# Earlier row counts, eight more 128-row tiles and moved matmuls in a recurrence fused with a mixture of experts

## The reference: what is computed

```python
xW = einsum('ntd,dh->nth', x, Wx) + b              # x: 2 sequences, 1024 steps, 256 wide
h[t] = tanh(xW[t] + h[t-1] @ Wh)                   # 1024 steps, one after the other
logits = h.reshape(2048, 256) @ gate_w.T           # 8 experts
top_v, top_i = top_k(logits, 2); probs = softmax(top_v)
for e in range(8):                                 # inner width 1024
    hidden = silu(h @ wg[e].T) * (h @ wu[e].T)
    out += combine[e] * (hidden @ wd[e].T)         # combine is 0 where e was not chosen
return x + out
```

## Time and profile before

| what | value |
|---|---|
| median of three runs | 864.16 us |
| the profiled execution's own time | 867.19 us |
| its span, first to last instruction | 865.4 us |
| TensorE matmuls busy | 803.9 us, 93% of the span |
| granted TensorE clock, mean | 0.903 |
| loads of expert rows (two for a pair) | 86 |

### The profile page before, as it was taken

How to read it: one execution, slowest core, us unless ns; L and a number is a source line. 1 busy time by engine, 2 the same in 40 slices (tenths; PEclk the granted TensorE clock), 3 DMA queues, 4 the chain that set the end, 5 groups by cost and what they waited for, 6 DMA issues and landing times.

```text
span 865.4 us, 53138 instructions
## 1 busy us (share of the span) xinstructions
PE 803.9 (93%) x22592; PEld 773.2 (89%) x22592; DVE 455.6 (53%) x2595; ACT 537.1 (62%) x2864; POOL 154.0 (18%) x142
## 2 busy tenths in 40 slices
PE   7777777899999999999999999999999999998994
PEld 4666666799999999999999999999999999998994
DVE  4677676545545454545454544545454545455552
ACT  4777787556666666666665666666665666654552
POOL 1001001010301121110302030212222131314332
PEclk7555555599999999999999999999999999999998
DMA  6667667411111111111201120112111111112211
GB/s 174 169 183 195 181 173 197 152 29 22 36 22 29 27 32 28 29 26 19 42 15 35 22 41 16 31 27 34 24 26 27 23 31 20 30 24 40 33 28 24
DMA packets 36021, 50.07 MB, mean 58 GB/s; under 512 B 5808, under 2 KB 22448, under 8 KB 35760
## 3 DMA queue, kind: packets, MB, share of 16 engines
q1 hardware_dynamic: 27408, 36.93, 15.5%
q0 software_dynamic: 8384, 9.84, 8.2%
HBM read 35.71 MB, written 13.14 MB: 56 GB/s over the span
## 4 chain that ended last, share of the span: by engine, by line
PE 81%; DMA 6%; DVE 4%; ACT 4%; issue 3%; SPq 0%; DVEq 0%; POOLq 0%; ACTq 0%
PE bank L506 27%; PE bank L424 18%; PE bank L583 15%; PE bank L528 13%; DMA arena<-w_all 4%; PE bank L537 3%; ACT h L746 3%; DVE lo L1044 3%; PE bank L403 2%; PE bank L485 1%; DMA out<-y_sb,place_now 1%; PE bank L477 1%; ACT w_hi L731 1%; DVE w_lo L1019 1%; PE bank L446 0%
## 5 line engine op out<-in xcount | busy, mean ns | idle before, releaser
L1044 DVE TENSOR_TENSOR lo<-h,hi 128x4 f16<-128x4 f32 x1024 | 168.2, 164 | 355.1 <-ACT h L746 339.4
L738 ACT ACTIVATE hi<-bank 128x4 f16<-128x4 f32 x1024 | 177.5, 173 | 230.6 <-PE bank L424 201.1
L583 PE MATMUL bank<-lo,wh_hi 128*128 128x2 f16 x4096 | 258.1, 167 | 29.8 <-DVE lo L1044 26.5
L424 PE MATMUL bank<-hi,wh_hi 128*128 128x2 f16 x4096 | 251.8, 165 | 10.6 <-ACT hi L738 9.3
L424 PE MATMUL bank<-hi,wh_lo 128*128 128x2 f16 x4096 | 245.6, 163 | 0.8 <-issue 0.8
L583 PEld LDWEIGHTS bank<-lo,wh_hi 128*128 128x128 f16 x4096 | 174.9, 99 | 45.8 <-DVE lo L1044 42.5
L424 PEld LDWEIGHTS bank<-hi,wh_hi 128*128 128x128 f16 x4096 | 200.0, 99 | 17.8 <-ACT hi L738 12.4
L746 ACT ACTIVATE h<-bank 128x4 f32<-128x4 f32 x1024 | 178.1, 174 | 32.8 <-PE bank L583 29.7
L424 PEld LDWEIGHTS bank<-hi,wh_lo 128*128 128x128 f16 x4096 | 177.7, 97 | 1.0 <-issue 0.9
L506 PE MATMUL bank<-x_T,w_hi 128*128 128x64 f16 (+1 forms) x2304 | 168.6, 202 | 2.2 <-DVE arena L972 1.5
L506 PE MATMUL bank<-x_T,w_lo 128*128 128x64 f16 (+1 forms) x1152 | 154.1, 202 | 0.0
(11 more groups left out here) (140 smaller groups left out, 1208.8 us busy)
## 6 DMA issues: line engine op xcount, KB each, us to landing
arena<-w_all SPq DMA_DIRECT2D x96, 256.0 KB, 2.9
xrow<-expert_rows SPq DMA_DIRECT2D x86, 66.0 KB
early<-xT SPq DMA_DIRECT2D x16, 128.0 KB, 2.9
expert_rows<-pad SPq DMA_DIRECT2D x1, 1056.0 KB, 8.6
expert_rows<-rows,slot POOLq DMA_INDIRECT x64
out<-y_sb,place_now POOLq DMA_INDIRECT x36, 3.2
out<-y_sb,place_wide POOLq DMA_INDIRECT x24
arena<-wh_in SPq DMA_DIRECT2D x1, 256.0 KB, 2.9
```

The source lines that it names most:

```text
L424: mm = pe.matmul(preact(n)[:, B * m:B * m + B], w[:, k, m * P:(m + 1) * P], hi[:, blk % 2, k, B * tt:B * tt + B], start=False, stop=False, ...
L583: mm = pe.matmul(preact(n)[:, B * m:B * m + B], wh_hi[:, k, m * P:(m + 1) * P], lo[:, pi, k, B * pt:B * pt + B], start=False, stop=False, ...
L738: act.activation(hi[:, blk % 2, :, B * tt:B * tt + B], src, ACT.Tanh, scale=1 / SCALE).then_inc(s_hi, 1)
L1044: v.tensor_tensor(lo[:, i, :, B * tt:B * tt + B], h32[:, 4 * (tt % 2):4 * (tt % 2) + 4].rearrange("p (c b) -> p c b", c=2), hi[:, i, :, B ...
```

## The change

The count of a block moves from 4 steps behind its last scatter to 3 steps ahead of it, and the scatters move to o = 0, 3, 6 and 9. `WIDE` becomes 32, so that pairs 24 to 31 take 128 rows of one expert. `fewer` is worked out from `heavy`: a step with a turn of x or y, or with logits or turned rows, hands two units (one 128-column matmul, or two of 64) to the other step of its couple (n ^ 1), unless that one is heavy too. The slice of pair 35 is made in the last four steps. In the tail the last count and routing ticks come one job later, and the list in lots of 3, 3 and 2.

```diff
--- before.py
+++ after.py
@@ -35,14 +35,14 @@
 TICKS = 19
 START, PERIOD, HALF_T = 208, 24, 12
 R = 64
-WIDE = 24
+WIDE = 32
 UNITS, FIRST_UNITS, FIRST_STEPS = 14, 24, 6
 SILU_AT, HI_AT = (2, 8), (5, 11)
 MUL_AT, LO_AT = (4, 10), (6, 0)
 YT_AT, WEIGH_AT, X_OUT_AT = 12, (15, 18), (21, 22)
 Y_TURN_AT, X_TURN_AT = (13, 14), (19, 20)
 SLICE_AT, TAKE_AT, SHIFT_AT, PASS_AT = (7, 8, 9, 11), 19, (13, 14), 15
-ADD_AT, SCATTER_AT = (16, 22), (2, 5, 9, 12)
+ADD_AT, SCATTER_AT = (16, 22), (0, 3, 6, 9)
 EXTRA = 2
 
 
@@ -103,7 +103,7 @@
         return [m for m in range(n, n + 2 * PERIOD) if (m - START) % PERIOD in SCATTER_AT][:4]
 
     def count_step(blk):
-        return scatter_steps(blk)[3] + 4
+        return scatter_steps(blk)[3] - 3
 
     def slice_step(p):
         return START + (p - 1) * PERIOD + SLICE_AT[0]
@@ -538,11 +538,14 @@
                               start=False, stop=True, skip_group_check=True)
                     n -= 4
 
-            def tile(p, o):
+            def heavy(n):
+                return pair_of(n)[1] in Y_TURN_AT + X_TURN_AT or (n >= STEPS and n % STEPS in (0,) + TURN_ROWS_AT)
+
+            def tile(p, o, n):
 
                 half, w = divmod(o, HALF_T)
                 part, sub = divmod(w, 2)
-                fewer = HALF_T - 2 if o in Y_TURN_AT else HALF_T + 2 if o in (Y_TURN_AT[0] - 1, Y_TURN_AT[1] + 1) else HALF_T
+                fewer = HALF_T + 2 * (heavy(n ^ 1) - heavy(n))
                 n0, n1 = (2 * HALF_T - fewer, 2 * HALF_T) if sub else (0, fewer)
                 pq, hq = (p, 0) if half else (p - 1, 1)
                 t = pq if part in (2, 5) else p
@@ -585,7 +588,7 @@
                 mm.then_inc(s_pre, 1)
                 units = 0
                 if p >= 0:
-                    units += tile(p, o)
+                    units += tile(p, o, n)
                 if not last:
                     units += next_xw(blk, tt)
                 if blk:
@@ -1062,6 +1065,8 @@
                         route(1 - i, blk - 1, tick)
                     if n == count_step(blk):
                         count(blk - 1)
+                if n >= T - 4:
+                    make_slice(NPAIR + 1, n - (T - 4))
 
             v.memset(all1[:], 1.0).then_inc(s_c, 1)
             v.memset(seen[:], 0.0).then_inc(s_c, 1)
@@ -1133,15 +1138,14 @@
             hidden_lo(NPAIR - 1, 1, 1)
             for tick in range(3, 14):
                 route(1, g, tick)
-            whole_slice(NPAIR + 1)
 
             def count_and_place(n):
-                if n == 1:
+                if n == 2:
                     count(g)
                     for tick in range(15, 20):
                         route(1, g, tick)
-                if n >= 2:
-                    lists(2 * n - 4, 2 * n - 2)
+                if n >= 3:
+                    lists((0, 3, 6)[n - 3], (3, 6, 8)[n - 3])
 
             def list_and_slice(n):
                 if n == 0:
```

## The result

The changed kernel takes 845.03 us (median of four, 843.07 to 846.02) against 863.79 us for the kernel before, a ratio of 0.9777 (95% interval 0.9755 to 0.98). Run again on another chip it took 844.14 us against 865.05, 0.9757 (0.9743 to 0.977). The prediction was 843.5 us, range 839 to 850. By medians the gain is 18.8 us the first time and 20.9 the second. The profiled execution took 846.02 us, 21.2 us less than the profiled one of before; the sum of terms had been 21.3.

The account below looks back on a forecast made before the run. TensorE's instruction stream was taken as the bound, with narrow code arriving too slowly. Terms 9.5 + 7.1 + 4.2 + 0.5 = 21.3 us gave 842.9 us against the median; a little less gain was taken: 843.5 us, range 839 to 850.

Parts of the forecast that it names:

- The sum: Whole kernel: 9.5 + 7.1 + 4.2 + 0.5 = 21.3 us less, taken as 843.5 us.
- What bounds the kernel: Whole kernel: TensorE's instruction stream, 81% of the chain of waits; narrow code is used up faster than it arrives.
- Part 1: Tail loop: by the count of rows five pairs in place of six, 84 loads for 86, saving 9.5 us.
- Part 2: Pairs 24 to 31 made wide: 6.3 us less there, 0.8 us in pairs 32 and 33, together 7.1 us.
- Part 3: Couples of steps hand a product over: turns of x, turned rows and logits shorten, 4.2 us together.
- fixed stock of 41 us: Narrow stretch: a stock of code carries it about 41 us before the first stall; pairs 32 and 33 need 35.
- "seventeen" steps: Pairs 26 to 31 of the kernel before: seventeen stalled steps above 0.88 us, many some 4.1 us apart.
- Part 4: Tail's order: times_up(34, 0, 1) ahead of last count and ticks, slice of pair 35 into steps; 0.5 us together.
- 0.4 us of the slice: Slice of pair 35, 0.9 us of VectorE, moves into steps; 0.4 us of it lay on the path.
- Part 5: Early count: in eight blocks load_pair waits for the last scatter's landing, but the load stays hidden by 1.5 us.
- The rival's price: Load late in eight periods: 851.5 us at 1 us late, slower than before above 2.6 us each; 5%, 2% slower.
- one of the prediction's signs of being wrong: Step o = 19, first reader of the expert rows: TensorE or VectorE waiting there for the load.

Follow-up runs that it names:

- the last run: Changed kernel with scatters at o = 0, 2, 4 and 6 and the last slot copy in a tick 20, run once more: 843.61 us, ratio 0.9739 to the kernel before.

## Why the prediction was right, point by point

**The sum.** That 21.3 met the 21.2 of the profiles so closely is in part luck. The steps from pair 1 on gave 11.8 us against 11.3, the tail 10.4 against 10.0, and the 1.0 us lost ahead of pair 1 stood in no term.

**What bounds the kernel**: TensorE's stream of instructions. Doubling the matmuls of eight pairs, and with them the weight loads, brought the stalls back, 8.3 us, and they end with the arrival of code. The Trainium skill, "Runtime: NRT & Kernel Launch", section "Instruction fetch mechanics", calls the crossing of a block mostly hidden. The traces agree for the wide code here (TensorE idle 0.02 us in 138.76) and not for the narrow (2.90 us in 105.06).

**Part 1, one pair fewer, 9.5 us**: right. The count from the routing gave 84, 88 and 84 loads for the three kernels that it was asked for. Beside the pair, the other pairs of the loop came 9.32 us apart in place of 9.46; with the rest of the tail that made 10.4. Why the spacing fell wasn't found: it is 9.27 to 9.39 us in the profiles with the narrow pairs, without the handover, with the late count and with the old tail too, so none of these makes it alone.

**Part 2, 7.1 us**: right in size, with part 3's share taken off: 7.5 - 1.0 in pairs 24 to 31, and 1.2 less 0.24 behind them. But what narrow code costs differs between kernels: 146.24 us in the kernel before, 143.34 with the pairs narrow again. Its premise of a fixed stock of 41 us was wrong: pairs 32 and 33 had no step above 0.86 us in the changed kernel, but stalls of 0.35 and 0.4 us, among others, in the last run. Of the "seventeen" steps above 0.88 us the starts of L746 show sixteen.

**Part 3, 4.2 us**: right, 4.05 in the traces, and of the 144 steps in pairs 1 to 31 that take a product 140 stay at or below 0.724; the other four are at 0.767, as before. Where both turns of x meet the turned rows (pairs 4, 12, 20 and 28) the two steps fall from 0.86 to 0.80 us only.

**Part 4, 0.5 us**: nothing came of it. The step that failed is "I get 0.3 us there by laying the durations end to end": TensorE's wait grew from 1.15 to 1.50 us, as ticks and list stand together ahead of the next product. For the 0.4 us of the slice no run shows a gain: ahead of the wait at 6.6 us TensorE has no idle time above 0.12 us in either tail. The clock's dip was not foreseen.

**Part 5, "hidden by 1.5 us"**: the size was off. From the issue of the last scatter of block 4 to the first load's issue I had 3.9 us, and from there to the end of the load 3.1. The changed kernel, on GpSimd, SyncE and TensorE:

```profile
229.39 0.90 POOL L1200 DMA_INDIRECT expert_rows<-rows,slot  x1 [1.25 <-ACT hi L741]
...
233.62 1.71 SPq L350 DMA_DIRECT2D xrow<-expert_rows  x2
...
237.92 0.29 PE L477 MATMUL bank<-ident,xrow 128*128 128x128 f16 x2
```

4.2 and 4.3 us. In six other profiles with this schedule the first was 4.4 to 4.9. In four of these profiles the packets show which terms were too small. The load is issued 1.35 to 1.45 us behind the scatter's last packet, where I had 0.8, which is what it takes behind the rows' place. Its last packet ends 3.2 to 3.6 us later, where I had 3.1, and the reader starts 0.7 to 0.8 us behind that, where I had nothing. The step at that turn was 0.774 us in this profile, and 0.93 to 1.11 in four others. One reads in the second run of the changed kernel

```profile
PEld bank L477 <- DMA xrow<-expert_rows: 0.2, 1, 0.2
```

For the other seven blocks the sum is nearly always within the 8.5 us that there are. From scatter to load they need mostly 3.0 to 3.3 us, two of them (5 and 10) often 3.9 to 4.5, and from the load's issue to a reader that had to wait it takes 3.8 to 4.4 us. So my estimate of the margin is nil for block 4, some tenths of a us for two blocks and about 1 us for the rest. The rival's price was wrong by far more: "slower if each is late by more than 2.6 us" supposed that a wait costs its length. So one of the prediction's signs of being wrong, TensorE waiting at o = 19 for the load, did show, at one block and for 0.4 us at most, too little to move the time.

## What to carry to other kernels

A unit's instructions are a resource of their own: where the same columns can be had from half as many matmuls, count the code blocks of the instruction queue a us, not only TensorE's busy time. Where a count comes before the data that it counts, measure the whole chain from the last write to the first reader in several executions, and give it the slack that costs nothing (here, the same four scatters three steps sooner), since one late load can cost the clock, here 27% of the time. A loop whose length follows from data is priced by working out the data: this one jumped between five, six and seven pairs with an edit that changed no work.

## What the runs showed of the hardware

A wait of 2.3 us took TensorE's clock to 1.2 GHz, and it stayed there for 440 us, with TensorE busy for 435.58 of 435.90 us. Idle times of up to 0.60 us in the steps never cost it, save on the chip below, and 1.15 or 1.5 us followed 7 us later by 2.1 or 2.2 us cost 3.41 us of it in five profiles of ten.

TensorE's instructions come in packets of 16 KB. At 54 matmuls and weight loads a us TensorE was idle 0.13 us in 139.90. At 67 to 69 a us it stalled, and eight pairs took 8.3 us more in the worst case, with a packet every 3.87 us.

One chip differed: in the run with scatters by o = 6 most of the steps in which GpSimd issued a DMA took 1.5 to 1.7 us and the next one 0.73, on ScalarE's timeline here 1.70 and 0.72:

```profile
242.15 0.17 ACT L749 ACTIVATE h<-bank 128x4 f32<-128x4 f32 x1
...
243.85 0.17 ACT L749 ACTIVATE h<-bank 128x4 f32<-128x4 f32 x1 [0.56 <-PE bank L586]
...
244.57 0.17 ACT L749 ACTIVATE h<-bank 128x4 f32<-128x4 f32 x1 [0.23 <-PE bank L586]
```

On the others such steps take 0.717. The cause wasn't found; with it the kernel before took 1082 to 1149 us there. The changed kernel wasn't run on that chip.
